# Adding the last two units' states in PSUM instead of with GpSimd, with passes re-ordered, in a 16-image conv and state-space kernel

## The chip, the core and the metric

The program runs on one core of a Trainium2 chip. The time is the device time of one execution in microseconds. The kernel before took 3897.47 us in the median of three runs (3894.95 to 3903.98).

Engines are named as the profile names them: PE is TensorE, DVE is VectorE, ACT is ScalarE, POOL is GpSimd, and SP is the queue that issues the DMAs.

## The reference

There are 16 images of 256 channels and 32 x 32 points. Two layers are applied, each with a group normalisation in front and a residual sum behind:

```python
x = x + _L0_conv_ref(_gn(x), ...)   # a 7x7 depthwise convolution whose weights come from the image itself
x = x + _L1_conv_ref(_gn(x), ...)   # in-projection, a selective scan over three resolutions, gate, out-projection
```

The second layer projects to 128 channels (`f1`, 1024 points), halves the picture twice (`f2`, 256 points, `f3`, 64 points), and runs on each level a scan forward and one backward, with 16 states:

```python
dA = jnp.exp(delta[..., None] * A)
dBx = delta[..., None] * Bs[:, :, None, :] * xt[..., None]
h = h * da + dbx                       # for every point, 16 states
y = jnp.einsum('bdn,bn->bd', h, c) + xt * Dv
return _layernorm(y, g, be)            # over the 128 channels
```

The sum of the three levels is multiplied by `silu(z)` and projected back to 256 channels.

## The kernel before

Three images are in work at once. While image i is scanned, image j = i + 1 has its 7 x 7 convolution done on PE, and image m = i + 2 is loaded, normalised, and its convolution weights are found. `stages` writes this as a body of 37 units (k = 0 to 36) and a `bridge` between two bodies; the body of images 0 to 13 is one loop of 14 turns (`Fori`, L1610), with two bodies ahead of it and two behind. Every engine runs its own instructions in the order in which they are written, and waits on semaphores for the others. So the order in `unit`, `bridge` and `tail` of each engine, and the tables at L1544 to L1551, are the schedule.

A unit is a piece of the scan. Unit 0 is the 64-point level with all 16 states and both directions; units 1 to 4 are the 256-point level, four states each and both directions; units 5 to 20 are the 1024-point level forward, one state each, and units 21 to 36 backward. A product q is a unit in one direction: 42 in all, q = 40 and 41 are units 35 and 36. In a unit of the 1024-point level:

- SP loads the rows B and C of the state, spread over all partitions, 512 KB each, into `bb` (two buffers) and `cb` (three) (`get_b`, `get_c`). `get_b` of unit k waits for POOL's `bx` pass of unit k - 2, `get_c` waits until the products of unit k - 3 are weighed.
- POOL makes `bx = bb * u` (L1466). It does so one unit ahead.
- ACT makes the decays `exp(delta * A)` in the PSUM tile `slot_b`, in two halves (`decay`, L1283).
- DVE scans each half into `slot_c` (L598) and multiplies it with `cb` into `h`, one of three places (`weigh`, L607).
- POOL adds `h` onto the sum `y` of its direction (`gather`, L1501) one unit later.

In units 1 to 4 the second direction is weighed by POOL (L1478), and PE adds the weighed states through the centring matrix `cen` into PSUM (`flat_add`, L923). For the 1024-point level `norm_centre` (L907) multiplies `y` with `cen` when all is added: parts 4 and 5 of the normalisation are the two halves of the backward direction. They stand at the head of the bridge, since they need product 41, and write into `slot_b` and `slot_c`.

Between the scan's instructions stand: on PE the 98 taps of the convolution of image j, six matmuls each (L842), of which the first seven are made in the last unit and the bridge; on ACT the 14 rows of 14 diagonal matrices for these taps (`make_row`, L1161), the copies `keep_x` (L1181) and `copy_x` (L1188), and the chunks of `delta`; on DVE the statistics of the new image (`a_s0`, L466). `delta` and `u` are made in six chunks: PE projects (`chunk_bc`, `chunk_dt`), ACT copies the rows B and C out and starts a softplus (`chunk_rows` L1228, `chunk_exp` L1236 to L1243), DVE corrects it (`chunk_first` L534), ACT takes a logarithm (`chunk_log` L1249), DVE ends it (`chunk_last` L543, L545) and POOL adds (`chunk_low` L1436, L1438). Chunks 0 and 1 are in the bridge, 2 and 3 in units 0 to 3, 4 and 5 in units 11 to 16.

The bridge gives ACT also `y_start` (L1263, five passes that start `y` with `f * Dv`, the last thing before the loop's jump) and DVE the two `output` passes (L681), `silu_clip` (L550), and unit 0's scans.

## Time and profile before

| | |
|---|---|
| median of 3 runs | 3897.47 us |
| the profiled execution | 3897.22 us, of it the span 3895.4 us |
| mean granted PE clock | 0.896 of full |
| PE busy | 3129.9 us, 80% |
| DVE busy | 3016.8 us, 77% |
| ACT busy | 2696.6 us, 69% |
| POOL busy | 3086.7 us, 79% |
| from one loop turn to the next | 228 to 232 us |

In the rows further down the first number is the start in us from the start of the span, the second the time taken, then engine, line, operation and tiles, then how many instructions are merged. What stands in brackets is how long the engine had been idle before, and what ended that; "issue" is time in which it waited for nothing that the profile shows. A matmul of 32-bit numbers is recorded as two. Busy shares near 80% on three engines say that no engine alone is the bound: each is idle at some places, and the rows show which.

### The profile page before, as it was taken

What the parts mean: (1) busy time and instruction counts of PE and PEld (TensorE: products, weight loads), DVE (VectorE), ACT (ScalarE), POOL (GpSimd) and SP (SyncE); (2) the same over time, 40 slices, a digit from 0 to 9 for tenths busy, and PEclk for the clock granted to TensorE, in tenths of its full rate; (3) what the DMA queues carried; (4) which work ended last, traced back from release to release, by engine and by line L of the source; (5) the groups of instructions that cost most, each with busy time, mean ns of one, the idle gap of its engine ahead of it and who ended that gap; (6) DMA issues with size and microseconds to landing.
All of it is one profiled execution on the core that took longest, in us unless ns stands there. A gap on an engine that the chain in (4) does not pass through costs nothing.

```text
span 3895.4 us, 54301 instructions
## 1 busy us (share of the span) xinstructions
PE 3129.9 (80%) x13644; PEld 1584.7 (41%) x13644; DVE 3016.8 (77%) x3847; ACT 2696.6 (69%) x6662; POOL 3086.7 (79%) x1588
## 2 busy tenths in 40 slices
PE   6988887987878898788888878898787879878632
PEld 3544344443434444344444434444443444443210
DVE  1058788787888878788887888788788887888887
ACT  4467676767777687776768767676776767676542
POOL 0049789796978979798796978879697897969797
PEclk8999898998898999899999989899898989989765
DMA  1026455564555546454564645455464555636454
GB/s 45 1 99 212 165 181 184 181 206 140 202 168 180 200 156 207 155 193 163 186 212 142 210 147 196 168 193 204 139 213 160 185 179 180 208 132 215 166 197 166
DMA packets 187326, 665.46 MB, mean 171 GB/s; under 512 B 22736, under 2 KB 24672, under 8 KB 186976
## 3 DMA queue, kind: packets, MB, share of 16 engines
q1 hardware_dynamic: 186976, 661.47, 50.0%
q8 instruction: 137, 2.24, 0.3%
q14 instruction: 213, 1.74, 0.2%
HBM read 639.76 MB, written 21.63 MB: 170 GB/s over the span
## 4 chain that ended last, share of the span: by engine, by line
PE 21%; POOL 21%; issue 20%; ACT 16%; DVE 12%; DMA 8%; DVEq 1%; POOLq 1%; SPq 0%; ACTq 0%
PE pconv L842 12%; POOL bx L1466 11%; DMA bb<-bc_rows 8%; POOL y L1501 7%; ACT diag L1161 5%; DVE h L607 4%; DVE slot_c L598 3%; PE pm L851 2%; PE pm L923 2%; ACT slot_b L1283 2%; PE pm L869 1%; ACT a L1274 1%; POOL h L1496 1%; POOL delta L1436 1%; ACT es L1236 1%
## 5 line engine op out<-in xcount | busy, mean ns | idle before, releaser
L842 PE MATMUL pconv<-pad,diag 128*128 128x464 f16 (+11 forms) x9408 | 2083.3, 376 | 166.8 <-DVE xn L520 99.8
L842 PEld LDWEIGHTS pconv<-pad,diag 128*128 128x128 f16 x9408 | 919.7, 99 | 1312.9 <-issue 288.4
L1501 POOL TENSOR_TENSOR y<-y,h 128x1024 f32<-128x1024 f32 (+1 forms) x544 | 1229.4, 2260 | 153.0 <-DVE h L607 149.2
L1283 ACT ACTIVATE slot_b<-delta,nega 128x512 f32<-128x512 f32 (+1 forms) x1280 | 809.6, 641 | 746.2 <-DVE slot_c L598 608.4
L1466 POOL TENSOR_TENSOR bx<-bb,u 128x1024 f32<-128x1024 f32 x512 | 1220.4, 2385 | 9.7 <-DMA bb<-bc_rows 9.0
L598 DVE TENSOR_TENSOR_SCAN slot_c<-slot_b,bx 128x512 f32<-128x512 f32 (+1 forms) x768 | 783.9, 1043 | 225.1 <-POOL bx L1466 144.8
L607 DVE TENSOR_TENSOR h<-slot_c,cb 128x512 f32<-128x512 f32 x1152 | 773.2, 672 | 0.0
L598 DVE TENSOR_TENSOR_SCAN slot_c<-slot_b,slot_c,bx 128x512 f32<-128x512 f32 x512 | 663.2, 1295 | 67.4 <-ACT slot_b L1283 9.6
L1161 ACT ACTIVATE diag<-id,chi 128x128 f16<-128x128 f16 x1568 | 496.1, 387 | 9.0 <-PE pconv L842 9.0
L1161 ACT ACTIVATE diag<-id,clo 128x128 f16<-128x128 f16 x1568 | 496.1, 387 | 0.0
L923 PE MATMUL pm<-h,cen 128*128 128x256 f32 x1024 | 251.1, 389 | 12.9 <-POOL h L1478 6.5
L1469 POOL TENSOR_TENSOR bx<-bb,u 128x1024 f32<-128x1024 f32 x64 | 157.8, 2467 | 109.6 <-DMA bb<-bc_rows 108.3
L1478 POOL TENSOR_TENSOR h<-h,cb 128x1024 f32<-128x1024 f32 x64 | 150.8, 2357 | 98.1 <-DVE h L598 98.1
L923 PEld LDWEIGHTS pm<-h,cen 128*128 128x128 f32 x1024 | 195.7, 194 | 72.0 <-DVE h L607 16.4
L1436 POOL TENSOR_TENSOR delta<-delta,rs 128x512 f32<-128x512 f32 (+1 forms) x96 | 97.9, 1020 | 155.6 <-DVE rs L545 155.5
L598 DVE TENSOR_TENSOR_SCAN h<-slot_b,bx 128x256 f32<-128x256 f32 x256 | 161.5, 672 | 53.8 <-POOL y L1501 27.0
L893 PE MATMUL pm<-f,wdelta 128*128 128x512 f32 (+1 forms) x192 | 102.6, 619 | 85.7 <-ACT rows L1228 66.6
L1446 POOL TENSOR_TENSOR f<-f,lnw 128x98 f32<-128x98 f32 x16 | 6.2, 391 | 173.5 <-ACT f L1106 173.5
L851 PE MATMUL pm<-xg,wf 128*128 128x512 f32 x128 | 94.9, 911 | 54.2 <-ACT xg L1209 54.2
L746 PE MATMUL pconv<-sg,grp 128*128 128x8 f32 x32 | 9.3, 365 | 149.9 <-DVE sg L466 149.9
L883 PE MATMUL pm<-f,wbc 128*32 128x512 f32 (+1 forms) x192 | 93.2, 570 | 25.6 <-DVE o L641 13.7
L543 DVE TENSOR_TENSOR pm<-pm,rs 128x512 f32<-128x512 f32 x64 | 44.3, 692 | 86.7 <-ACT pm L1249 86.7
(182 smaller groups left out, 3250.1 us busy)
## 6 DMA issues: line engine op xcount, KB each, us to landing
bb<-bc_rows SPq DMA_DIRECT2D x592, 512.0 KB, 4.6
cb<-bc_rows SPq DMA_DIRECT2D x592, 512.0 KB, 4.4
xr<-in_x SPq DMA_DIRECT2D x16, 1024.0 KB, 5.0
out<-ob SPq DMA_DIRECT2D x16, 1024.0 KB
bc_rows<-rows SPq DMA_DIRECT2D x64, 64.0 KB, 3.2
w<-in_w SPq DMA_DIRECT2D x2, 256.0 KB
wc<-in_wc SPq DMA_DIRECT2D x2, 256.0 KB
bc_rows<-rows SPq DMA_DIRECT2D x16, 32.0 KB, 4.5
```

The lines of the kernel that those rows point to most:

```text
L598: ins = nc.vector.tensor_tensor_scan(hv, av, bv, start, ALU.mult, ALU.add)
L607: nc.vector.tensor_tensor(half(h[:, q % HR], b), bank(slot_c, b), half(cb[:, k % CR], b), ALU.mult).then_inc(q_pr.sem, 1)
L842: ins = nc.tensor.matmul(img(bank(pconv, k), W)[:, r0:r1, c0:c1], w, pad[:, t, part, 16 * k + r0 + dy:16 * k + r1 + dy, c0 + dx:c1 + dx], ...
L851: ins = nc.tensor.matmul(bank(pm, k), wf[:, t, :], bank(xg[:, t, :], k), start=(t == 0), stop=(t == CT - 1))
L923: ins = nc.tensor.matmul(pm[:, d * L2:(d + 1) * L2], cen[:, :], h[:, q % HR, n * L2:(n + 1) * L2], start=False, stop=n == 3 and q == FLAT[-1])
L1161: ins = nc.scalar.activation(diag[:, r % RING, m, dx, :], id16[:, :], ACT.Copy, scale=(chi, clo)[m][:, t, dy * KK + dx:dy * KK + dx + 1])
L1283: ins = nc.scalar.activation(slot_b[:, o:o + w], delta[:, so + c:so + c + w], ACT.Exp, scale=nega[:, st, n0 + n:n0 + n + 1])
L1436: pool.tensor_tensor(delta[:, s:s + n], delta[:, s:s + n], er[:, c % 2, 0:n], ALU.add).then_inc(ch_delta.sem, 1)
L1466: ins = pool.tensor_tensor(bx[:, k % 2, :], bb[:, k % BR, :], us, ALU.mult)
L1469: ins = pool.tensor_tensor(o, bb[:, k % BR, :].rearrange("p (m l) -> p m l", m=m), us[:, None, :].to_broadcast([P, m, ln]), ALU.mult)
L1478: pool.tensor_tensor(h[:, q % HR, 0:HW], h[:, q % HR, 0:HW], cb[:, k % CR, :], ALU.mult).then_inc(p_pr.sem, 1)
L1501: pool.tensor_tensor(yv, yv, src[:, 0] if len(src.shape) == 3 else src, ALU.add).then_inc(q_y.sem, 1)
```

## The change

PE takes over the last two products. `gather` on POOL no longer adds q = 40 and 41. `norm_centre` of parts 4 and 5 multiplies `y`, then `h` of product 40, then `h` of product 41 with `cen`, into the same PSUM place. The rest is order:

- SP: `get_b` and `get_c` of unit 2 stand in the bridge ahead of the output's DMA, no more in unit 0 behind it; the load of the next image (`xr`) goes from unit 2 to unit 5, behind `get_c` of unit 7.
- DVE: the statistics of `xr` go from unit 3 to units 8 and 9, half each; the passes of chunk 4 are one unit later.
- PE: `lower(j, 1)` and chunk 0's projections come ahead of the second convolution tap of the last unit.
- ACT: seven diagonals of row 0 one unit later, behind `decay` of unit 36; five diagonals of row 1 out of the last unit into the bridge behind `copy_z`; `keep_x` from unit 1 to 3, `copy_x` from 1 to 4; `a_xh_` from 12 to 14; the logarithms of chunks 3 to 5 earlier within their unit (4: in unit 14).
- POOL: in unit 5 `bx` of unit 6 comes ahead of the weighing of product 9; `f_affine` in unit 26 comes one pass earlier.

```diff
+LAST = (NP - 2, NP - 1)
 def added(q):
-    return sum(v not in FLAT for v in range(q + 1))
+    return sum(v not in FLAT and v not in LAST for v in range(q + 1))
...
 (SP, unit)
-                    if k + 2 < NU:
+                    if 2 < k + 2 < NU:
                         get_b(i, k + 2)
                         get_c(i, k + 2)
-                if k == 2 and j is not None and m is not None:
+                if k == 5 and j is not None and m is not None:
                     sp.dma_start(xr[:, :, :], xv[m]).then_inc(x_in.sem, 16)
 (SP, bridge)
                     get_c(j, 1)
+                    get_b(j, 2)
+                    get_c(j, 2)
 (PE, norm_centre)
-                nc.tensor.matmul(o, cen[:, :], src, start=True, stop=True).then_inc(n_yc.sem, 1)
+                if k >= 4:
+                    pe.wait_ge(q_h.sem, q_h.at(i, NHALF))
+                    if k == 5:
+                        pe.wait_ge(q_pr.sem, q_pr.at(i, weighed(NP - 1)))
+                ins = nc.tensor.matmul(o, cen[:, :], src, start=True, stop=k < 4)
+                if k >= 4:
+                    for q in LAST:
+                        pe.wait_ge(q_pr.sem, q_pr.at(i, weighed(q)))
+                        ins = nc.tensor.matmul(o, cen[:, :], h[:, q % HR, c0:c0 + n], start=False, stop=q == LAST[-1])
+                ins.then_inc(n_yc.sem, 1)
 (ACT, bridge, behind copy_z)
                 if m is not None:
+                    make_row(m, 1, 9)
                     make_row(m, RING - 2, 0, KK)
 (ACT, unit)
-                    if k == 1:
+                    if k == 3:
                         keep_x(i)
-                if j is not None and k == 1:
+                if j is not None and k == 4:
                     copy_x(j)
 (POOL, unit)
+                    if k == 5:
+                        inputs(i, k + 1)
                     for q in products_of(k - 1):
                         if q in POOLED:
                             weigh(i, q)
-                    if k + 1 < NU:
+                    if k + 1 < NU and k != 5:
                         inputs(i, k + 1)
...
-                            if q not in FLAT:
+                            if q not in FLAT and q not in LAST:
                                 gather(i, q)
...
-pre = {3: a_s0, 18: a_max_, ...}
+pre = {8: a_s0, 9: a_s1, 18: a_max_, ...}
-CHUNK_FIRST = {(1, -4): 2, (2, -1): 3, (13, -1): 4, (15, -1): 5}
-CHUNK_LOG = {2: 3, 13: 4, 15: 5}
+CHUNK_FIRST = {(1, -4): 2, (2, -1): 3, (14, -2): 4, (15, -1): 5}
+CHUNK_LOG = {2: 3, 15: 5}            # chunk 4: at the head of unit 14
```

On PE at the head of the bridge stood, from the projection of the 64-point level on (`f` and `wc`) to chunk 1 (`wbc` with 256 columns):

```order
L869 MATMUL pm<-f,wc 128x64 [waits b_f]
L869 MATMUL pm<-f,wc 128x64 x3
L875 REGISTER_ALU
L883 MATMUL pm<-f,wbc 32x64 [waits b_f]
L893 MATMUL pm<-f,wdelta 128x64
L903 REGISTER_ALU
L907 MATMUL slot_b<-y,cen 128x512 [waits q_y]
L907 MATMUL slot_c<-y,cen 128x512 [waits q_y]
L877 ISA
L883 MATMUL pm<-f,wbc 32x256 [waits ch_rows]
```

With the change a convolution tap (`pconv`, its last two of six matmuls are shown) stands between chunk 0 and the centring, and the centring has six matmuls:

```order
L850 MATMUL pconv<-pad,diag 128x13x30
L850 MATMUL pconv<-pad,diag 128x16x30
L911 REGISTER_ALU
L916 ISA [waits q_y]
L919 MATMUL slot_b<-y,cen 128x512 [waits q_h]
L922 REGISTER_ALU
L923 MATMUL slot_b<-h,cen 128x512 [waits q_pr]
L922 REGISTER_ALU
L923 MATMUL slot_b<-h,cen 128x512 [waits q_pr]
L919 MATMUL slot_c<-y,cen 128x512 [waits q_pr,q_h,q_y]
L923 MATMUL slot_c<-h,cen 128x512 [waits q_pr] x2
L885 ISA
```

Chunk 1's projection (L883, now L891) stands behind four more matmuls.

On ACT in the bridge, from the 64-point level's decays (`a`) over `copy_z` (`sz`) to the diagonals of row 2 (`diag` from `chi`):

```order
L1274 ACTIVATE a<-delta,nega 128x64 x15
L1219 REGISTER_ALU [waits b_g]
L1220 ACTIVATE sz<-pm,vec 128x1024 [waits b_proj]
L1161 ACTIVATE diag<-id,chi 128x128 [waits row_done]
L1161 ACTIVATE diag<-id,chi 128x128 x6
```

And with the change, where the five `clo` diagonals of row 1 come in between:

```order
L1290 ACTIVATE a<-delta,nega 128x64 x15
L1235 REGISTER_ALU [waits b_g]
L1236 ACTIVATE sz<-pm,vec 128x1024 [waits b_proj]
L1177 ACTIVATE diag<-id,clo 128x128 x5
L1177 ACTIVATE diag<-id,chi 128x128 [waits row_done]
L1177 ACTIVATE diag<-id,chi 128x128 x6
```

All that follows on ACT, `y_start` with it, is five instructions further back, and five fewer stand ahead of chunk 0.

On ACT in unit 1 and 2, from the end of chunk 3's softplus start (`pm` from `es`) to its logarithm (`pm` from `pm`):

```order
L1243 ACTIVATE pm<-es 128x512 [waits ch_pos,ch_exp]
L1181 ACTIVATE xc<-xn 128x2048 [waits ob_ready]
L1187 REGISTER_ALU [waits b_xc]
L1188 ACTIVATE xn<-xr 128x2048 [waits b_xg]
L1279 REGISTER_ALU
L1283 ACTIVATE slot_b<-delta,nega 128x256 [waits q_h]
L1283 ACTIVATE slot_b<-delta,nega 128x256
L1161 ACTIVATE diag<-id,clo 128x128 x3
L1156 REGISTER_ALU
L1161 ACTIVATE diag<-id,chi 128x128 [waits row_done]
L1161 ACTIVATE diag<-id,chi 128x128 x2
L1249 ACTIVATE pm<-pm 128x512 [waits ch_err]
```

And with the change:

```order
L1259 ACTIVATE pm<-es 128x512 [waits ch_pos,ch_exp]
L1295 REGISTER_ALU
L1299 ACTIVATE slot_b<-delta,nega 128x256 [waits q_h]
L1299 ACTIVATE slot_b<-delta,nega 128x256
L1265 ACTIVATE pm<-pm 128x512 [waits ch_err]
L1177 ACTIVATE diag<-id,clo 128x128 x3
L1172 REGISTER_ALU
L1177 ACTIVATE diag<-id,chi 128x128 [waits row_done]
```

The logarithm of chunk 3 has only one `decay` ahead of it; the two copies and six diagonals that stood there come behind.

## Rows read from the trace of the kernel before

**Rows 1.** The timeline of DVE, `silu_clip` of three loop turns: start, us, line

```profile
1160.48 1.28 DVE L550 TENSOR_SCALAR o<-pm,vec 128x1024 f32<-128x1024 f32 x1
...
1392.48 1.28 DVE L550 TENSOR_SCALAR o<-pm,vec 128x1024 f32<-128x1024 f32 x1
...
1621.26 1.28 DVE L550 TENSOR_SCALAR o<-pm,vec 128x1024 f32<-128x1024 f32 x1
```

**Rows 2.** The timeline of PE from the last unit to unit 1

```profile
1373.37 1.34 PE L842 MATMUL pconv<-pad,diag 128*128 128x390 f16 x6
...
1376.45 1.08 PE L907 MATMUL slot_b<-y,cen 128*128 128x512 f32 x2
1377.36 1.02 PE L907 MATMUL slot_c<-y,cen 128*128 128x512 f32 x2
...
1388.17 1.88 PE L938 MATMUL slot_b<-o,wo 128*128 128x512 f32 x4
...
1399.25 1.98 PE L842 MATMUL pconv<-pad,diag 128*128 128x406 f16 x6 [3.13 <-issue]
...
1410.43 1.02 PE L893 MATMUL pm<-f,wdelta 128*128 128x512 f32 x2
```

**Rows 3.** The timeline of ACT, bridge to unit 13

```profile
1375.80 1.56 ACT L1161 ACTIVATE diag<-id,clo 128x128 f16<-128x128 f16 x5
...
1399.53 3.26 ACT L1263 ACTIVATE y<-f,vec 128x1024 f32<-128x1024 f32 x5
...
1466.64 0.59 ACT L1228 ACTIVATE rows<-pm 32x512 f32<-32x512 f32 x1 [1.27 <-PE pm L883]
...
1477.55 2.36 ACT L1142 ACTIVATE xh<-xr,sa 128x1024 f32<-128x1024 f32 x2
```

**Rows 4.** The timeline of DVE, units 1 to 13

```profile
1406.33 1.27 DVE L598 TENSOR_TENSOR_SCAN h<-slot_b,bx 128x256 f32<-128x256 f32 x2 [2.35 <-POOL y L1501]
...
1422.02 0.70 DVE L543 TENSOR_TENSOR pm<-pm,rs 128x512 f32<-128x512 f32 x1 [4.32 <-ACT pm L1249]
...
1429.23 2.44 DVE L466 BATCH_NORM_STATS2 sa<-xr 128x6 f32<-128x512 f32 x4
...
1477.65 0.69 DVE L534 SCALAR_TENSOR_TENSOR rs<-pm,es 128x512 f32<-128x512 f32 x1 [2.62 <-ACT pm L1243]
...
1482.38 0.70 DVE L543 TENSOR_TENSOR pm<-pm,rs 128x512 f32<-128x512 f32 x1 [2.26 <-ACT pm L1249]
```

**Rows 5.** The timeline of POOL, end of a body to unit 13

```profile
1372.65 3.19 POOL L1501 TENSOR_TENSOR y<-y,h 128x1024 f32<-128x1024 f32 x1 [0.23 <-DVE h L607]
...
1399.94 2.73 POOL L1469 TENSOR_TENSOR bx<-bb,u 128x1024 f32<-128x1024 f32 x1 [7.03 <-DMA bb<-bc_rows]
...
1439.91 4.68 POOL L1466 TENSOR_TENSOR bx<-bb,u 128x1024 f32<-128x1024 f32 x2
...
1447.42 2.36 POOL L1466 TENSOR_TENSOR bx<-bb,u 128x1024 f32<-128x1024 f32 x1 [0.51 <-DMA bb<-bc_rows]
...
1485.69 2.35 POOL L1501 TENSOR_TENSOR y<-y,h 128x1024 f32<-128x1024 f32 x1 [3.48 <-DVE h L607]
```

**Rows 6.** A window (PE, PEld, DVE, ACT, POOL, clock, DMA, GB/s); `bb`'s landings

```profile
1420.00:1428.00 8.00, 8.00 (x38) 4.97 (x36) 5.95 (x10) 6.52 (x20) 4.98 (x4) 1.00 0.93 328
...
DMA to landing us min/median/max: 3.3/4.6/7.2
```

**Rows 7.** The timeline of PE at slow jumps, then DVE behind one

```profile
937.96 2.43 PE L842 MATMUL pconv<-pad,diag 128*128 128x406 f16 x6 [5.87 <-issue]
...
3008.40 2.43 PE L842 MATMUL pconv<-pad,diag 128*128 128x406 f16 x6 [4.38 <-issue]
...
1185.07 1.27 DVE L598 TENSOR_TENSOR_SCAN h<-slot_b,bx 128x256 f32<-128x256 f32 x2 [3.61 <-PE pm L923]
```

**Rows 8.** PE at the end of the last image; then the window there, columns as in rows 6

```profile
3876.01 2.08 PE L907 MATMUL slot_b<-y,cen 128*128 128x512 f32 x2 [22.56 <-POOL y L1501]
...
3876.00:3881.00 5.00, 4.99 (x6) 2.11 (x7) 0.00 (x0) 1.19 (x2) 0.00 (x0) 0.50 0.00 0
```

More of the change, by code:

```diff
@@ L461, in _, with stats @@
             dve.wait_ge(setup, DVE_SET + ACT_SET)
-            def stats(b, s, x, done):
-                for t in range(CT):
+            def stats(s, x, ts):
+                for t in ts:
                     for k in range(2):
                         ins = nc.vector.bn_stats(s[:, 12 * t + 6 * k:12 * t + 6 * k + 6], bank(x[:, t, :], k))
-                ins.then_inc(done.sem, 1)
+                return ins
             def a_s0(m):
@@ L471, in a_s0, with a_s1 @@
                 dve.wait_ge(x_in.sem, x_in.at(m + 1, 0))
-                stats(m, sa, xr, a_stats)
+                stats(sa, xr, (0,))
+            def a_s1(m):
+                stats(sa, xr, (1,)).then_inc(a_stats.sem, 1)
             def low_half(j, t):
@@ L1006, in unit @@
                         lower(j, 0)
-                    if m is not None:
-                        taps(m, BRIDGE_TAPS[1], BRIDGE_TAPS[2])
-                    if j is not None:
                         lower(j, 1)
@@ L1012, in unit @@
                         chunk_dt(j, 0)
+                    if m is not None:
+                        taps(m, BRIDGE_TAPS[1], BRIDGE_TAPS[2])
                 if m is not None and k in pre:
@@ L1355, in tail @@
                     make_row(m, 0, 0, KK)
-                if k == PREP + 1:
-                    if j is not None:
-                        b_normal(j)
+                if j is not None and k == PREP + 1:
+                    b_normal(j)
+                if k == PREP + 2:
                     if m is not None:
                         make_row(m, 0, KK)
-                if k == PREP + 2:
-                    if m is not None:
                         prep(m, 1)
@@ L1374, in tail @@
                         copy_f(j, 2)
-                    if m is not None:
-                        make_row(m, 1, 9)
             def unit(i, j, m, k):
@@ L1382, in unit @@
                 if i is not None:
[L1383 to L1384 removed]
+                    if k in (1, 14):
+                        chunk_log(i, {1: 2, 14: 4}[k])
                     if k == 11:
@@ L1390, in unit @@
                         decay(i, k + 1, 0)
+                    if k in CHUNK_LOG:
+                        chunk_log(i, CHUNK_LOG[k])
                 if m is not None and k == PREP:
@@ L1515, in unit @@
                             weigh(i, q)
-                    if k + 1 < NU:
+                    if k + 1 < NU and k != 5:
                         inputs(i, k + 1)
+                if m is not None and k == 26:
+                    f_affine(m)
+                if i is not None:
                     for v in (k - 1, k) if k == NU - 1 else (k - 1,):
                         for q in products_of(v):
-                            if q not in FLAT:
+                            if q not in FLAT and q not in LAST:
                                 gather(i, q)
```

16 lines of the change are left out of this document (5 added, 11 removed).

## The prediction

> **What bounds the kernel now.** I read the timelines of one loop turn, engine by engine, with what ended each idle time; shares of the whole span do not help, since the bound changes within a turn. First DVE's `silu_clip`, which stands once in each turn: the turns are 232.0 and 228.8 us long [rows 1], so there are two kinds. I work through the short one from 1392 on and return to the long one.
>
> In units 7 to 33 POOL is the bound: two passes of about 2.35 us per unit back to back, with one hole of 3.48 us at unit 14 [rows 5], where DVE comes late because it stood idle 2.62 and 2.26 us for ACT's chunk 4 [rows 4]. ACT in turn came late there: its copy of the rows waited 1.27 us for PE, and 2.36 us of `xh` stood before its next work [rows 3]. So PE's place in its own queue matters at unit 11, through ACT. In the bridge and units 0 to 5 no engine is full. PE runs without a hole from the centring at 1376.45 to the jump, after which 3.13 us pass; POOL's last `y` ends at 1372.65 + 3.19 = 1375.84, 0.6 us before the centring starts [rows 2, 5]. So POOL's last two passes are hardly what the bridge waits for: PE got there only then. DVE then waits 2.35 us for POOL's first `y`, which needs `y_start`, ended on ACT at 1399.53 + 3.26 = 1402.8, and 4.32 us for the logarithm of chunk 3 [rows 3, 4].
>
> **The bridge: a loss.** The two POOL passes go, but what replaces them stands on the engine that is full. Four matmuls more: two in a row start 0.91 us apart [rows 2], 4 x 0.91 = 3.6 us. From below nothing is excluded only if PE has a hole there, and it has none; from above, each could take the 2.08 us that the pair at the granted clock of 0.50 took in the last image [rows 8], 8.3 us. I take 3.6, because the same place ran at 0.91. The tap that moves in front of the centring takes about 1.2 us (1.34 less the overlap into the next), of which 0.4 comes back because the 64-point projection no longer stands behind it [rows 2]: 0.8. Out-projection and everything behind it on PE start 3.6 + 0.8 = 4.4 us later, DVE's outputs too, since they wait for it. The stall that the change removes for POOL, 7.03 us for the third `bb` of the bridge [rows 5], was in front of work that waited for `y_start` anyway: worth nothing. `decay` of unit 36 comes 2.0 us earlier on ACT (seven diagonals less ahead), and the last product with it: nothing behind it waits for it any more, so nothing.
>
> On ACT the bridge's chain hangs on PE's spread, so +4.4; the five diagonals of 1.56 us [rows 3] now stand ahead of `y_start`, where before they filled a wait; about 0.8 us comes back from DVE's chunk 1 pass, which then runs without a POOL pass beside it. `y_start` ends at 4.4 + 1.6 - 0.8 = 5.2 us later, POOL's first `y` follows, and DVE's scan at 1406.33 [rows 4] starts 5.2 us later.
>
> **Units 1 to 6: a gain of the same size.** The logarithm of chunk 3 stood on ACT behind two copies (3.8 us) and six diagonals (1.9 us). Now it has one `decay` ahead, and 4.32 us of DVE's wait [rows 4] go; 0.5 to 0.9 us of other small waits in these units are absorbed by the lateness. Unit 3 starts on DVE at +0.2. The statistics, 2.44 us in unit 3 [rows 4], no longer stand ahead of the scans for which POOL waits; and in unit 5 `bx` of unit 6 comes ahead of a weighing, so it comes about 2.5 us earlier than 1439.91 [rows 5]. POOL's sum of passes is the same, so its `bx` of unit 8 would be free to start at 1446.6 instead of 1447.42 [rows 5].
>
> It has to wait for its data, though. `get_c` of unit 7 waits for the weighing of product 9, now behind one pass more (+2.1 us), then the 1 MB of `xr` is issued, and only then `get_b` of unit 8. In the window with `xr` in it the queues moved 328 GB/s at a DMA share of 0.93 [rows 6]; 1 MB in front costs 3.2 us more. The 512 KB take 4.6 us as a rule, and 7.2 at most [rows 6]. Issued at 1443.2, they land at about 1450: +2.7 us against 1447.42.
>
> PE is late too. Chunk 3's projection (1410.43, [rows 2]) moves by 4.2; of it PE gets back 0.8 in small holes until unit 5, then it has none until unit 13: +3.4 at unit 10 and 11, where ACT waited for it already [rows 3].
>
> **Units 8 to 16: the lateness is paid back.** ACT's rows of chunk 4 at 1466.64 come 3.4 us later. `xh` (2.36 us) stands two units further back, the logarithm too, and DVE asks for chunk 4 a unit later, so its waits of 2.62 and 2.26 us go, 4.9 us. The moved statistics cost DVE 2.44 us in units 8 and 9, hidden by its slack against POOL. Followed through: ACT's chunk 5 comes 0.9 us earlier than before, DVE's unit 16 at -0.2, and POOL has two holes of about 0.8 instead of one of 3.48. POOL's `bx` of unit 18 starts at 3.48 - 2.7 - 0.8 + ~0.2 = -0.2 us. From there to the bridge nothing changes. A turn is worth -0.2 us, 14 turns -3 us. It is the difference of about 8 us lost and 8 us won; each part is good to 1 us, the whole to 3.
>
> **The long turns.** Where the jump cost PE 4.4 to 5.9 us instead of 3.1 to 3.6 (five of 14), DVE waited 3.61 us for PE in unit 2 [rows 7], and the turn was about 3.1 us longer. At the jump 2 MB are under way: output, third `bb` and `cb`. With the change the latter two have landed. If that is what slows the jump, up to 5 x 3.1 = 15.5 us go; if not, none. I take half, -8.
>
> **The last images.** Images 14 and 15 have no diagonals and no statistics: the bridge's loss comes with less to gain, +3 in all. At the very end PE adds 40 and 41 itself; its `y` part can start before product 41 is weighed: -2.3 for the POOL pass, + two to three matmuls at the low clock, between 0 and +4; I take 0.5.
>
> The Trainium skill, page "TensorE: Matmul & The Clock Gate", Part 1, says that the throttled clock is the default and activity releases it; the trace agrees, PE comes out of 22.56 us of idleness at a granted clock of 0.50 [rows 8]. By that rule the added matmuls cost double in the last image only, since in the loop's bridge PE comes to them at work, and its pair stood 0.91 us apart [rows 2]; the sum would be the same.
>
> The page "GPSIMD Engine Reference", section "Specifications", says that GpSimd shares its SBUF interfaces with VectorE when that has two SBUF inputs. The trace agrees: the `y` pass beside such a DVE pass took 3.19 us, another 2.35 [rows 5]. By it the early third `bx` runs against DVE's 64-point scans and lengthens them by about 1 us, ahead of a wait of 3 us: nothing in the sum.
>
> **The sum.** The profiled execution took 3897.22 us, 1.8 us more than its span, and is 0.25 us under the median. 3897.2 - 3 - 8 + 3 + 0.5 = 3889.7; I say 3890.
>
> **The rivals.**
> Slower: the repayment in units 8 to 16 fails. ACT starts its work for chunk 4 3.4 us late, POOL 2.7 us late; if DVE's waits there come back in another place (for chunk 5, or for the decays behind `xh` in unit 14), the hole of 3.48 us stays and the turn is 3.0 us longer: 14 x 3.0 + 3.5 = +45, 3942; decided from where ACT ends chunk 5's start later than before. For it: ACT has no hole between units 11 and 13, and PE's lateness goes straight into it. Against it: 2.9 us of ACT's work leave that stretch. Half of it gives 3920.
>
> Clearly faster: PE's lateness is not there, because PE's jump is short and the rest of its waits in units 0 to 5 (0.8 us and those for POOL's weighed states) hold more slack than I found. Then the whole hole of 3.48 goes, the turn is worth -2.5 to -3, and long turns vanish: -14 x 2.5 - 8 = 3854. Against it: PE is full from 1412 on.
>
> No gain in the long turns and none in the short: the two POOL passes were off the path, so the change doesn't do what it says; the rest cancels: 3897 to 3901.
>
> **How the numbers follow.** The forecast's own range is 3875 to 3903, chance 0.4; slower 0.27; clearly faster 0.18; no change at all 0.15. What a measurement of this kernel tells from no change is about 0.2%, 8 us. The forecast lies at its edge: of its 0.4, 0.23 is faster, 0.12 the same, 0.05 slower. Faster 0.23 + 0.18 + 0.02 = 0.43, same 0.12 + 0.11 = 0.23, slower 0.05 + 0.27 + 0.02 = 0.34. The range 3850 to 3936 leaves out a tenth at either end.
>
> **What would show it.** Right if: PE's out-projection comes 4 to 5 us later after the last unit; the five diagonals stand before `y_start`, and DVE waits about 3 us for POOL's first `y` (2.35 before); no wait of DVE for `pm` L1249 of chunk 3; POOL's hole before `bx` of unit 8 is 3 us or more; DVE's two waits at chunk 4 are gone and the POOL hole at unit 14 is under 2 us; fewer turns over 231 us. Wrong if the centring starts earlier than 0.5 us before its old place, if `bx` of unit 8 waits for nothing, or if ACT comes to unit 14 as late as to unit 11.

## The result, and the profile after

The changed kernel took 3935.15 us (median of 5 runs, 3933.52 to 3940.14) against 3898.51 us for the kernel before beside it: a ratio of 1.0086, 95% interval 1.0072 to 1.0100. On another chip, later, the same kernel took 3933.39 us against 3914.85, a ratio of 1.0039 (1.0023 to 1.0054). (The ratios are worked out from all executions, so they are not the quotients of the medians.) It is slower both times; what is known of why the ratio differs stands below. The forecast was 3890 us and slightly faster. The time lies at the upper end of its range, and the sign was wrong.

The page of the profile after, its first lines and the groups of GpSimd and VectorE that answer to the prediction (line engine op, count, busy and mean ns, idle before and its releaser):

```profile
span 3938.3 us, 54525 instructions
...
PE 3220.4 (82%) x13772; PEld 1622.5 (41%) x13772; DVE 3008.5 (76%) x3847; ACT 2694.4 (68%) x6662; POOL 2995.9 (76%) x1556
...
L1479 POOL TENSOR_TENSOR bx<-bb,u 128x1024 f32<-128x1024 f32 x512 | 1222.6, 2388 | 69.5 <-DMA bb<-bc_rows 69.4
L1514 POOL TENSOR_TENSOR y<-y,h 128x1024 f32<-128x1024 f32 (+1 forms) x512 | 1143.4, 2233 | 63.0 <-DVE h L615 59.3
L606 DVE TENSOR_TENSOR_SCAN slot_c<-slot_b,bx 128x512 f32<-128x512 f32 (+1 forms) x768 | 783.6, 1043 | 260.4 <-POOL bx L1479 227.4
L1509 POOL TENSOR_TENSOR h<-h 128x512 f32<-128x512 f32 (+3 forms) x128 | 86.8, 678 | 147.0 <-ACT y L1279 139.5
L1449 POOL TENSOR_TENSOR delta<-delta,rs 128x512 f32<-128x512 f32 (+1 forms) x96 | 98.1, 1022 | 377.1 <-DVE rs L553 377.1
```

POOL is 76% busy and less than before, since its two passes per image are gone, and the kernel is slower: the idle time in front of `delta` rose from 155.6 us to 377.1, by more than the 86 us of the passes that are gone, in a place where POOL waits for the bridge anyway. Of the 69.4 us in front of `bx` only 9.0 were there before.

`silu_clip` again, which stands once in each turn:

```profile
1409.29 1.27 DVE L558 TENSOR_SCALAR o<-pm,vec 128x1024 f32<-128x1024 f32 x1
...
1641.43 1.28 DVE L558 TENSOR_SCALAR o<-pm,vec 128x1024 f32<-128x1024 f32 x1
```

A turn is 232.14 us long where the short turn was 228.8 [rows 1]. Over the 14 turns the median is 232.2, with three of 234.3 to 235.1. The mean, 232.75, is 2.7 us over that of before (230.04, short and long turns together): 14 x 2.7 = 38 us. The last body is 3.3 us longer too; the first `silu_clip` comes 2.9 us later (243.12 against 240.21), and what follows the last one is 1.2 us shorter: 43 us between the two spans. The 2.9 us are not shown to be the change's: in a later profile of the same kernel (after2) the first `silu_clip` stands at 239.84.

In what follows 12.7 us are taken off times of the changed kernel's turn at 1371 to 1603 to lay it on the turn of rows 1 to 5: GpSimd's pass for `y` that waits 2.92 us for `h` stands at 1371.27 in one and 1358.57 in the other.

TensorE in the bridge:

```profile
1388.71 1.34 PE L850 MATMUL pconv<-pad,diag 128*128 128x390 f16 x6
1389.89 1.02 PE L919 MATMUL slot_b<-y,cen 128*128 128x512 f32 x2
1390.74 1.88 PE L923 MATMUL slot_b<-h,cen 128*128 128x512 f32 x4
1392.46 1.02 PE L919 MATMUL slot_c<-y,cen 128*128 128x512 f32 x2
1393.32 1.88 PE L923 MATMUL slot_c<-h,cen 128*128 128x512 f32 x4
1395.13 0.62 PE L891 MATMUL pm<-f,wbc 128*32 128x256 f32 x2
...
1404.99 1.88 PE L955 MATMUL slot_b<-o,wo 128*128 128x512 f32 x4
...
1415.88 2.43 PE L850 MATMUL pconv<-pad,diag 128*128 128x406 f16 x6 [2.95 <-issue]
```

The added matmuls take 1392.46 - 1390.74 = 1.72 and 1395.13 - 1393.32 = 1.81 us, 3.5 together. The out-projection stands at 1404.99 - 12.7 = 1392.3, 4.1 us later than before [rows 2]; 4.4 was forecast.

GpSimd from unit 7 on:

```profile
1464.70 2.35 POOL L1479 TENSOR_TENSOR bx<-bb,u 128x1024 f32<-128x1024 f32 x1 [4.74 <-DMA bb<-bc_rows]
...
1504.93 2.36 POOL L1514 TENSOR_TENSOR y<-y,h 128x1024 f32<-128x1024 f32 x1 [0.62 <-DVE h L615]
...
1574.74 0.37 POOL L1465 TENSOR_TENSOR wlo<-wg,whi 128x98 f16<-128x98 f32 x1 [1.32 <-ACT whi L1140]
```

The hole of 3.48 us at unit 14 [rows 5] is down to 0.62 here (0.87 in the median of the 14 turns), as forecast. In its place there are two others: 4.74 us for `bb` of unit 8, and 1.32 for ACT's `whi` in unit 28.

### The profile page after: what moved, and what is told of

Same layout as the page of the kernel before. It is cut to its first block, busy times and chain, and to the rows that moved or that the text cites. A ratio compares the mean times of both kernels' runs of the same rounds, so it can differ in the third digit from the quotient of the medians.

```text
span 3938.3 us, 54525 instructions
## 1 busy us (share of the span) xinstructions
PE 3220.4 (82%) x13772; PEld 1622.5 (41%) x13772; DVE 3008.5 (76%) x3847; ACT 2694.4 (68%) x6662; POOL 2995.9 (76%) x1556
## 4 chain that ended last, share of the span: by engine, by line
PE 23%; POOL 23%; issue 18%; DMA 12%; DVE 11%; ACT 11%; DVEq 1%; SPq 1%; POOLq 0%; ACTq 0%
POOL bx L1479 13%; DMA bb<-bc_rows 12%; PE pconv L850 11%; POOL y L1514 7%; DVE h L615 4%; ACT diag L1177 3%; DVE slot_c L606 3%; PE pm L859 2%; PE pm L940 2%; ACT a L1290 1%; PE pm L877 1%; POOL h L1491 1%; DVE h L606 1%; PE pm L891 1%; ACT slot_b L1299 1%
## 5 line engine op out<-in xcount | busy, mean ns | idle before, releaser
L850 PE MATMUL pconv<-pad,diag 128*128 128x464 f16 (+11 forms) x9408 | 2123.1, 381 | 123.8 <-DVE xn L528 67.6
L850 PEld LDWEIGHTS pconv<-pad,diag 128*128 128x128 f16 x9408 | 931.1, 101 | 1288.1 <-issue 320.1
L1479 POOL TENSOR_TENSOR bx<-bb,u 128x1024 f32<-128x1024 f32 x512 | 1222.6, 2388 | 69.5 <-DMA bb<-bc_rows 69.4
L1514 POOL TENSOR_TENSOR y<-y,h 128x1024 f32<-128x1024 f32 (+1 forms) x512 | 1143.4, 2233 | 63.0 <-DVE h L615 59.3
L1449 POOL TENSOR_TENSOR delta<-delta,rs 128x512 f32<-128x512 f32 (+1 forms) x96 | 98.1, 1022 | 377.1 <-DVE rs L553 377.1
L1509 POOL TENSOR_TENSOR h<-h 128x512 f32<-128x512 f32 (+3 forms) x128 | 86.8, 678 | 147.0 <-ACT y L1279 139.5
L891 PE MATMUL pm<-f,wbc 128*32 128x512 f32 (+1 forms) x192 | 92.5, 566 | 58.7 <-DVE o L649 45.6
```

The source lines that it names most:

```text
L850: ins = nc.tensor.matmul(img(bank(pconv, k), W)[:, r0:r1, c0:c1], w, pad[:, t, part, 16 * k + r0 + dy:16 * k + r1 + dy, c0 + dx:c1 + dx], ...
L891: nc.tensor.matmul(bank(pm, 1 if c == 5 else 0)[0:2 * NS, 0:n], wbc[:, st, :], f[:, fc:fc + n], start=True, stop=True).then_inc(ch_bc.sem, 1)
L1479: ins = pool.tensor_tensor(bx[:, k % 2, :], bb[:, k % BR, :], us, ALU.mult)
L1514: pool.tensor_tensor(yv, yv, src[:, 0] if len(src.shape) == 3 else src, ALU.add).then_inc(q_y.sem, 1)
```

## The experiments

A turn's length tells more than a ratio of medians, since the kernel before took between 3898 and 3921 us by the chip. So each trial has both; the turn is the median of the 14 distances between `silu_clip`s in its profile, with the mean behind it. In several kernels turns come in two lengths; there the median jumps from one to the other, and the mean is the better guide. Where kernels of different chips are compared, a few microseconds prove nothing.

| kernel | turn, us: median, mean | median time, us | ratio to before beside it |
|---|---|---|---|
| before, and again as before2 | 229.2, 230.0; 232.2, 232.0 | 3898.5; 3915.8 | 1; 0.9986 |
| changed (two chips) | 232.2, 232.8; 232.4, 233.0 | 3935.2; 3933.4 | 1.0086; 1.0039 |
| b_last | 233.4, 233.7 | 3961.6 | 1.0126 |
| a_pooladd | 228.8, 229.4 | 3881.8 | 0.9913 |
| a_xrearly | 229.4, 230.1 | 3903.9 | 0.9985 |
| a_unswap | 230.4, 230.6 | 3901.6 | 0.9969 |
| a_wlow29 | 231.4, 231.3 | 3920.0 | 1.0010 |
| a_tinyxr | 231.7, 230.9 | 3910.5 | 0.9997 |
| a_taps | 231.6, 231.3 | 3918.6 | 1.0003 |
| c_early | 226.7, 226.9 | 3850.4 | 0.9827 |
| c_early_wlo | 225.3, 225.5 | 3834.7 | 0.9795 |
| c_unswap_wlo | 225.3, 225.6 | 3832.7 | 0.9785 |
| d_diag | 225.3, 225.3 | 3828.7 | 0.9782 |
| d_early | 225.3, 225.5 | 3832.7 | 0.9791 |
| d_taps | 224.5, 224.3 | 3816.4 | 0.9748 |
| e_taps_diag | 224.1, 224.0 | 3812.6 | 0.9734 |
| b_load | 228.7, 229.1 | 3887.7 | 0.9925 |

**The matmuls alone, and all but the matmuls.** The first is the kernel before with this alone (`LAST` and `added` as in the change):

```diff
+                if k >= 4:
+                    for q in LAST:
+                        pe.wait_ge(q_pr.sem, q_pr.at(i, weighed(q)))
+                        ins = nc.tensor.matmul(o, cen[:, :], h[:, q % HR, c0:c0 + n], start=False, stop=q == LAST[-1])
...
-                            if q not in FLAT:
+                            if q not in FLAT and q not in LAST:
                                 gather(i, q)
```

> The kernel before with one part of the change alone: TensorE adds the states of units 40 and 41 in PSUM, GpSimd's two passes go, nothing is re-ordered. Theory (the bridge's loss is the four added matmuls and carries through, because GpSimd is full from unit 5 on and nothing here takes away its hole of 3.48 us at unit 14): about +3.6 us in the bridge, all of it kept, 14 x 3.6 = +50, near 3948 us; at least +30. Rival (the added matmuls are covered, and the loss of the changed kernel comes from its re-ordering alone): within 10 us of the kernel before, 3890 to 3908.

The second is the changed kernel with this, and the waits of `norm_centre` that hang on it:

```diff
-LAST = (NP - 2, NP - 1)
+LAST = ()
```

> The changed kernel with its re-ordering kept, but units 40 and 41 added by GpSimd again as before (two passes more, four matmuls less). Theory (matmuls cost 3.6 us per turn in the bridge, on the path): TensorE's out-projection, VectorE's outputs and everything to unit 8 come about 3.6 us earlier, 14 x 3 to 3.6 = -42 to -50 us, 3885 to 3893 us, faster than the kernel before. Rival (the loss sits in the burst of transfers at unit 8 and in the wait for wlo, the matmuls are covered): 3930 to 3940, as the changed kernel.

Both went as the theory had it: b_last stands 1.3% over the kernel before, which is the +50 us expected, though on a chip where the kernel before itself took 3912.9 us; a_pooladd is 53 us under the changed kernel, a little more than the 42 to 50. Two rows of `silu_clip`, first of b_last, then of a_pooladd:

```profile
1409.49 1.28 DVE L553 TENSOR_SCALAR o<-pm,vec 128x1024 f32<-128x1024 f32 x1
...
1641.58 1.27 DVE L553 TENSOR_SCALAR o<-pm,vec 128x1024 f32<-128x1024 f32 x1
```

```profile
1388.06 1.28 DVE L558 TENSOR_SCALAR o<-pm,vec 128x1024 f32<-128x1024 f32 x1
...
1616.83 1.28 DVE L558 TENSOR_SCALAR o<-pm,vec 128x1024 f32<-128x1024 f32 x1
```

With the matmuls alone a short turn is 232.1 us, 3.3 over 228.8. Without them the changed kernel has short turns of 228.8, 3.4 less than with them. So the exchange costs nearly the whole length of the matmuls (3.5 us) in both surroundings, and the two POOL passes give next to nothing back. The re-ordering by itself leaves a short turn exactly as long as it was. The forecast had it win 3.8 us.

**The transfer of xr.** Three trials on the changed kernel. SyncE's queue in the changed kernel itself:

```profile
1455.34 0.32 SPq L403 DMA_DIRECT2D cb<-bc_rows  x1
1455.92 0.39 SPq L432 DMA_DIRECT2D xr<-in_x  x1
1456.42 0.40 SPq L403 DMA_DIRECT2D bb<-bc_rows  x1
1456.93 0.41 SPq L403 DMA_DIRECT2D cb<-bc_rows  x1
1457.66 0.32 SPq L403 DMA_DIRECT2D bb<-bc_rows  x1
```

Three megabytes are asked for within 2.3 us. The first four of these transfers stood behind one wait for POOL's weighing, which ends at 1455.3; the last was let go by the `bx` pass that ends at 1457.6. The `bb` at 1456.42 is the one for which POOL waits; it lands 8.1 us later (7.8 to 8.7 over the 14 turns). First, `xr` out before the wait:

```diff
                 if 2 < k + 2 < NU:
                     get_b(i, k + 2)
+                if k == 5: ... xr ...
                     get_c(i, k + 2)
-                if k == 5: ... xr ...
```

> The changed kernel with one transfer in another place: xr (1 MB) is issued between get_b(7) and get_c(7), so as soon as copy_x has read it (1452.0 in the changed kernel's trace) instead of behind get_c(7) at 1455.9. Theory (bb of unit 8 landed 8.5 us after its issue because xr was put out 0.5 us ahead of it): it lands 4.6 to 6 us after its issue at about 1455.9, GpSimd's wait of 4.74 us falls to 1.0 to 2.5, and 2 to 3.5 us per turn are won: 3888 to 3908 us. Rival (bb of unit 8 is bound by something else, or TensorE's lateness takes over at unit 11): under 1 us per turn, 3921 to 3935.

Second, POOL's passes of unit 5 in their old order:

```diff
-                    if k == 5:
-                        inputs(i, k + 1)
                     for q in products_of(k - 1):
...
-                    if k + 1 < NU and k != 5:
+                    if k + 1 < NU:
```

> The changed kernel with the exchange on GpSimd in unit 5 undone: the weighing of unit 5 runs ahead of bx of unit 6 again. Then get_c(7), and what stands behind it on the queue (xr, bb of unit 8), is no longer held by the pass in between: get_c(7) and xr 2.3 us earlier, bb of unit 8 0 to 1 us earlier (it then waits for bx of unit 6 itself). Theory (the exchange made the burst): GpSimd's wait for bb of unit 8 falls by 1 to 2.5 us, 3900 to 3921 us. Rival (the burst is xr's alone and the exchange is neutral, VectorE's scan of unit 6 then waits longer for bx): 3930 to 3945.

Third, `xr` in its place with 8 of its 1024 columns per half, which leaves out nearly all of this input:

```diff
-                    sp.dma_start(xr[:, :, :], xv[m])
+                    sp.dma_start(xr[:, :, 0:8], xv[m][:, :, 0:8])
```

> The changed kernel with xr's transfer in its place, but 8 KB of it in place of 1 MB (the rest of xr keeps what it held, so this input is left out). Theory (most of GpSimd's 4.74 us for bb of unit 8 is the megabyte ahead of it, the rest the late issue behind get_c(7)): the wait falls to 1 to 2 us, 2.8 to 3.5 us per turn, 3885 to 3898 us. Rival (the late issue at 1456.4 alone does it, three transfers at once being slow anyway): it stays above 3.5 us, 3920 to 3935 us.

The pass that waits, of the three in this order:

```profile
1678.03 2.36 POOL L1479 TENSOR_TENSOR bx<-bb,u 128x1024 f32<-128x1024 f32 x1 [2.10 <-DMA bb<-bc_rows]
```

```profile
1441.79 2.36 POOL L1479 TENSOR_TENSOR bx<-bb,u 128x1024 f32<-128x1024 f32 x1 [1.49 <-DMA bb<-bc_rows]
```

```profile
1450.04 2.35 POOL L1479 TENSOR_TENSOR bx<-bb,u 128x1024 f32<-128x1024 f32 x1 [2.75 <-DMA bb<-bc_rows]
```

The 4.74 us fall to 2.10, 1.49 and 2.75. The first two confirm the place of the loss and bring 2.8 and 1.8 us per turn by the medians. By the means it is 2.6 and 2.1 us, by the times 2.2 and 2.4, so the two remedies are worth the same within what can be told. In a_unswap the wait fell by 3.2 us, more than the 1 to 2.5 expected: `bb` goes out 1.1 us earlier (46.0 instead of 47.1 us behind `silu_clip`), and lands in 5.9 us though `xr` is still 1.7 us ahead of it.

The third misses both expectations: without its megabyte the wait is 2.0 us shorter, not 2.8 to 3.5, and `bb` still takes 6.1 us to land (5.0 to 7.5 by the turn), with `cb`, `bb` and `cb` issued within two microseconds. With both remedies together (d_early, further down) it lands in 4.4 us and POOL does not wait. From these differences I estimate three parts of the wait: the megabyte (2.0 us), the other transfers close by (6.1 - 4.4 = 1.7) and the later issue (1.1).

The mean turn of a_tinyxr is 1.9 us shorter than that of the changed kernel, which is the 2.0 us of the wait; its median hides it. Five of its turns are 228.8 to 229.1 us and nine 231.3 to 232.4. In the five POOL does not wait for `wlo` at all; in eight of the nine it waits 1.34 to 1.41 us. That is part of the difference; the rest I did not follow.

**wlo.** One unit later:

```diff
-                    if k == 28:
+                    if k == 29:
                         w_low(m)
```

> The changed kernel with GpSimd's small pass for wlo one unit later (29 instead of 28), behind two more passes of 2.35 us. Theory (wlo's wait of 1.32 us for ACT's whi is on GpSimd's path in each turn, as nothing but GpSimd sets the pace there): the wait goes and the turn is 1.3 us shorter, 14 x 1.3 = 18 us, 3910 to 3925 us. Rival (the wait is covered: VectorE or TensorE at the end of the turn sets the time, and the hole appears again as a longer wait of 2.92 us for VectorE's h at unit 32): 3930 to 3938.

The turn is 0.8 us shorter by the median and 1.45 by the mean, the time 15 us shorter than the changed kernel's 3935 (and 13 than its 3933): most of the 18 us expected. The clearer proof is the next pair.

**Do the terms add?**

> The changed kernel with GpSimd adding units 40 and 41 again, and xr issued ahead of get_c(7): both losses removed, the re-ordering kept. Theory (the two losses are separate terms of one sum): the gain of the one (about 4 us per turn, measured) and the gain of the other (2.8 us per turn, measured) add, turns of about 226 us, ratio to the kernel before 0.9913 - 0.0101 = 0.981, 3820 to 3830 us at 3898 for before. Rival (a turn has a floor of 228.7 us that another engine sets, since short turns of the kernel before and of both single trials have that length): 3855 to 3875.

> As the last, with the pass for wlo in unit 29 too. Theory (terms add): 1.3 us per turn less, ratio about 0.976, 3800 to 3815 us. Rival (the floor of 228.7 us per turn): 3850 to 3875; a rival between them: TensorE comes nearer to the end of GpSimd's turn and only half of it shows, 3815 to 3830.

> The changed kernel with GpSimd adding units 40 and 41, the exchange of passes in unit 5 undone instead of the earlier xr, and wlo in unit 29. Theory: GpSimd still waits about 1.5 us for bb of unit 8 (as with the exchange alone undone) against 2.1 with the earlier xr: within 10 us of the last kernel, 3800 to 3820 us. Rival (the earlier bx of unit 6 is worth something to VectorE): 10 us or more slower than it.

They add, nearly. `xr` early takes a_pooladd's 228.8 to 226.7, `wlo` in unit 29 takes that to 225.3: 2.1 and 1.4 us. The ratio of c_early is the 0.981 expected within its interval; c_early_wlo came to 0.9795 (0.9771 to 0.9820) where full addition gave 0.976, so some microseconds of the sum are missing. All three took longer than their ranges in microseconds, which had been worked out for a kernel before of 3898 us; beside them it took 3917. There is no floor of 228.7 us; that several kernels had turns of that length was chance. The old order in unit 5 is worth as much as the early `xr`.

**What else the re-ordering holds.** Three edits to c_unswap_wlo: the five diagonals of row 1 back in the last unit, `xr` early too, TensorE's bridge in its old order:

```diff
                         lower(j, 0)
+                    if m is not None:
+                        taps(m, BRIDGE_TAPS[1], BRIDGE_TAPS[2])
+                    if j is not None:
                         lower(j, 1)
                         chunk_bc(j, 0)
                         chunk_dt(j, 0)
-                    if m is not None:
-                        taps(m, BRIDGE_TAPS[1], BRIDGE_TAPS[2])
```

> The fastest kernel so far (changed kernel, GpSimd adds 40 and 41, exchange in unit 5 undone, wlo in unit 29) with the five diagonals of row 1 back from the bridge to the last unit. Theory (they stand ahead of y_start for 1.6 us, and GpSimd's first y pass waits 9.2 us for y_start): VectorE's scan in the bridge comes 1.2 to 1.6 us earlier, and about 1 us of it per turn is kept, 10 to 20 us faster than 0.9785 of the kernel before, a ratio of 0.974 to 0.976. Rival (they delay ScalarE's chunk 0 at the end of the turn by as much, where it stands between VectorE's two chunk passes): 0.978 to 0.982.

> The fastest kernel so far with xr issued ahead of get_c(7) too. Theory (the remaining 1.5 us of wait for bb of unit 8 is xr's megabyte directly ahead): xr goes out about 1.5 to 2 us earlier, the wait falls below 0.8 us, 0.5 to 1.3 us per turn, ratio 0.974 to 0.977. Rival (bb of unit 8 is issued when bx of unit 6 is done and the wait is its own landing): within 5 us of 0.9785.

> The fastest kernel so far with TensorE's order in the bridge as in the kernel before: three taps between the two projections of lower, so one tap less ahead of the centring and the taps ahead of chunk 0's projections. Theory (the new order is worth nothing or a little: the tap in front cost 0.8 us, chunk 0 comes earlier): within 0.5 us per turn, ratio 0.977 to 0.981. Rival (the new order carries a large part of the gain, since chunk 0's start on ScalarE and VectorE is on the bridge's chain): 1.5 us or more per turn slower, ratio above 0.984.

The diagonals and the second remedy for `xr` gave nothing that can be told from the interval (0.9782 and 0.9791 against 0.9785). For `xr` the profile says why. POOL's wait for `bb` of unit 8 (1.6 us in the median of c_unswap_wlo) is gone, and some 20 us later POOL waits as long for DVE:

```profile
1430.57 1.27 DVE L471 BATCH_NORM_STATS2 sa<-xr 128x6 f32<-128x512 f32 x2
...
1435.47 1.27 DVE L471 BATCH_NORM_STATS2 sa<-xr 128x6 f32<-128x512 f32 x2
...
1444.97 2.35 POOL L1514 TENSOR_TENSOR y<-y,h 128x1024 f32<-128x1024 f32 x1 [1.57 <-DVE h L615]
```

From 1418 to 1444 DVE has no hole above 0.3 us: the statistics that the change moved to units 8 and 9, with the normalisation passes beside them, fill it. TensorE's order, which I had expected to be worth nothing, gave 0.8 us per turn by the median and about 1.2 by the mean and by the time (16 us). One tap in front of the centring was put at 0.8; the edit also moves the taps against chunk 0's projections, so how much is the tap's is not told apart. That was tried on the changed kernel too, and the diagonals again without that tap:

> The changed kernel itself again, on the chip of the next two. The kernel before took 3898 to 3917 us by the chip, so a difference between single trials of other calls is good to 0.4% only. Theory: turns of 232.1 us with a few longer ones whatever the chip, 3930 to 3942 us, ratio 1.004 to 1.009. Rival (the change gets its whole 0.9% from the first chip, on which the kernel before had fewer long turns): ratio under 1.004.

> The changed kernel with TensorE's order in the bridge as before (one tap less ahead of the centring, three taps between the two projections of lower), the rest changed. Theory (the new order costs the 0.8 us of the tap in front and delays what hangs on the centring, as it did in the fast version, where undoing it won 0.4%): 0.5 to 1.3 us per turn, 7 to 18 us faster than the changed kernel. Rival (in the changed kernel its cost is covered by GpSimd's other waits): within 4 us of it.

> The fastest kernel (GpSimd adds 40 and 41, exchange in unit 5 undone, wlo in unit 29, TensorE's bridge as before) with the five diagonals of row 1 back in the last unit too. Theory (undoing the diagonals won 4 us, not beyond its interval; with TensorE's order undone ScalarE's start of y is next on the chain): 0.5 to 1 us per turn more, 3802 to 3812 us. Rival (covered): 3812 to 3820 us.

On one chip the old order makes the changed kernel 15 us faster (3918.6 against 3933.4), within the 7 to 18 expected. The diagonals bring 0.4 us per turn now by the profiles of two chips; the intervals of the two ratios overlap (0.9717 to 0.9751 and 0.9727 to 0.9770), so this gain is not shown. At 3812.6 us it stands between theory and rival. e_taps_diag is the fastest kernel of all, 2.7% under the kernel before. It keeps the change's other moves: the earlier logarithm and later chunk 4, `xh` in unit 14, the statistics in units 8 and 9, `bb` and `cb` of unit 2 in the bridge.

**The long turns.** The kernel before again, and with the third loads of the bridge alone ahead of the output:

```diff
                     get_b(j, 1)
                     get_c(j, 1)
+                    get_b(j, 2)
+                    get_c(j, 2)
                 if i is not None:
                     sp.wait_ge(ob_ready.sem, ob_ready.at(i + 1, 0))
```

> The kernel before itself with a profile, beside the next. On its first chip 6 of its 14 turns took 230.5 us or more. Theory (its time by the chip, 3898 to 3917 us, is the number of long turns, 3.1 us each): at 3910 us or more it has 8 to 12 long turns, short ones still of 228.3 to 229.3. Rival (all its turns are longer on another chip): short turns above 229.5 us.

> The kernel before with one part alone: bb and cb of unit 2 are asked for in the bridge, ahead of the output, instead of behind it in unit 0. Theory of the forecast (the long turns come from a loop jump under the load of output, third bb and cb): the long turns go, up to 3.1 us each, 15 to 30 us faster than before2. Rival (the long turns are set by TensorE's own place relative to what it waits for, not by these transfers): as many as in before2, within 6 us of it.

In this profile all 14 turns of the kernel before are long, 230.9 to 232.8 us; I had expected 8 to 12, and short ones beside them. The profiled execution is the slowest of ten (3925.0 us; their median is 3915.8), so in most of the others some turns will have been short. With the loads moved, 12 of 14 turns are 228.2 to 229.3, and the kernel is 28 us faster by the medians (0.9925, interval 0.9903 to 0.9948), within the 15 to 30 expected. A short turn is as long as in the kernel before (228.7 and 228.8), so the gain is not that `bb` lands earlier. TensorE behind the loop's jump, of before2 and of b_load in the same turn:

```profile
713.28 2.43 PE L842 MATMUL pconv<-pad,diag 128*128 128x406 f16 x6 [6.32 <-issue]
```

```profile
704.84 2.38 PE L844 MATMUL pconv<-pad,diag 128*128 128x406 f16 x6 [3.00 <-issue]
```

The thirteen jumps take 3.8 to 6.3 us in before2, 3.1 to 5.9 in the first profile of before [rows 7], and 2.8 to 3.2 in b_load, as in the changed kernel. So most long turns of the kernel before come from jumps beside these transfers (four of the six in the first profile; the other two follow no slow jump), and the change does away with them. How many there are differs from execution to execution, and its medians differ from chip to chip, 3898 to 3921 us. This fits the loss of 0.9% on one chip and 0.4% on the other: the changed kernel's own time is the same (3935 and 3933), and the kernel before was slower beside the second. No profile of it was taken on that second chip, so its long turns there were not counted.

In the first profile of the kernel before, POOL waits 1.33 to 1.38 us for `wlo` in five of the six long turns and at most 0.42 in the short ones; in b_load it waits 1.34 in a turn of 231.8 us and at most 0.47 in the others. So this wait is part of what a long turn consists of.

There is a second kind of long turn, which the trials with short jumps still have: 3 of 14 in a_pooladd, more in some others. The same stretch of TensorE's second half in a short and in a long turn of a_pooladd (window, busy of PE, PEld, DVE, ACT and POOL, granted clock, DMA share, GB/s):

```profile
1480.00:1500.00 20.00, 16.52 (x61) 6.84 (x62) 16.16 (x20) 14.39 (x29) 18.95 (x11) 0.84 0.49 177
1500.00:1520.00 20.00, 16.37 (x85) 9.00 (x83) 18.39 (x22) 13.65 (x33) 20.00 (x10) 0.90 0.64 232
...
1938.00:1958.00 20.00, 17.37 (x59) 7.44 (x60) 16.23 (x20) 14.40 (x29) 18.88 (x11) 0.76 0.52 173
1958.00:1978.00 20.00, 16.38 (x75) 8.56 (x74) 18.34 (x22) 13.80 (x32) 20.00 (x10) 0.84 0.64 229
```

The granted clock is lower there, 0.76 and 0.84 against 0.84 and 0.90, behind a hole of 4.67 us that both turns have. Why one turn gets less than another, no run tells. That it makes the turn long was read from these rows and not tested.

## Why the prediction was wrong, step by step

**The bridge, right.** 3.6 us for the matmuls (3.5 in the trace, 3.3 to 3.4 in two trials), 0.8 for the tap (0.8 to 1.2 in d_taps, with what else its edit moves), outputs 4.4 later (4.1). That the POOL passes were not on the path held in both trials. The diagonals in front of `y_start` were put at 1.6 us; undoing them gave nothing that stands clear of the intervals. DVE waits 2.39 us for POOL's first `y`, where about 3 was the sign. The 64-point scans, said to become 1 us longer beside the early `bx`, took 5.10 us instead of 4.53. POOL's first `y`, forecast 5.2 us later, came 4.7 later:

```profile
1423.75 1.27 DVE L606 TENSOR_TENSOR_SCAN h<-slot_b,bx 128x256 f32<-128x256 f32 x2 [2.39 <-POOL y L1514]
```

1423.75 - 12.7 = 1411.05 against 1406.33 [rows 4].

**Units 1 to 6, right up to the transfer.** The wait of 4.32 us for chunk 3's logarithm [rows 4] is gone. POOL is free for `bx` of unit 8 at 1464.70 - 4.74 - 12.7 = 1447.3, 0.7 us after the forecast.

**The landing of bb for unit 8, the first step that failed.** The forecast has two terms, 3.2 us for the megabyte and 4.6 for the transfer, from an issue at 1443.2. They make 7.8 and a landing at 1451.0; the text says about 1450, +2.7 us, which is 6.8 and drops a microsecond. The issue came at 1443.7 and the landing took 8.1: `bx` at 1452.0, +4.6 us. Of the 1.9 us between, 1.0 is that slip in the sum, 0.5 the later issue, and 0.3 the landing. That the landing itself is so near 7.8 is luck, since both terms were off: the megabyte costs 2.0, and without it `bb` takes 6.1, because the step asked what stands directly ahead of the transfer and not what else is let go beside it.

**Units 8 to 16, right in the main.** The rival for "slower" was that this lateness isn't repaid at chunks 4 and 5. ACT's copy of the rows of chunk 4 waited 1.33 us for PE, much as before [rows 3], and came 5.0 us later than before (3.4 was forecast). But DVE's waits of 2.62 and 2.26 us [rows 4] are down to this one, and 0.56 us for a decay behind it:

```profile
1495.46 0.69 DVE L542 SCALAR_TENSOR_TENSOR rs<-pm,es 128x512 f32<-128x512 f32 x1 [0.62 <-ACT pm L1259]
```

POOL's hole of 3.48 us is 0.62 too. The rival's own sign, ACT ending the start of chunk 5 later than before, did come (by 0.5 us, where 0.9 earlier was forecast), but the hole did not stay. So the time came out near that rival's 3942, but not by its mechanism.

**"From there to the bridge nothing changes", the second step that failed.** From unit 14 on POOL runs closer behind PE and ACT than before, because its hole there went and theirs did not. In unit 28 it meets their chain for the weights of the next image:

```profile
1570.06 0.49 ACT L1131 ACTIVATE wg<-pm,vec 128x49 f32<-128x49 f32 x2 [2.95 <-PE pm L804]
```

ACT waits for PE's product, and `wlo` on POOL for ACT: 1.32 us, 1.4 by the trial. The matmuls are not to blame: a_pooladd has the same wait (1.38). Nor is it new: before2 has 1.34 to 1.38 us there in nine of its 14 long turns. I had seen that wait in a long turn and had not asked when a short one would get it.

**The sum.** Forecast for a short turn: 3.6 + 0.8 + the rest, -0.2. Measured: +3.3. The two failed steps, 4.6 - 2.7 = 1.9 and 1.3 to 1.4, are 3.3 of the 3.5 us between. The second term is the weaker one: in after2 four turns have no wait for `wlo` and are as long as the others (231.6 to 232.6 us); in three of them POOL had waited 5.5 to 6.0 us for `bb` of unit 8, where 4.8 is the median. So the two overlap in part.

**The long turns, right in mechanism.** The forecast counts five turns behind jumps of 4.4 to 5.9 us; the profile has four, and two more long turns without one. I gave half of 15.5 us to it; on the first chip the mean of the turns stands 1.25 us above a short turn in before and 0.6 in the changed kernel, which has three longer turns beside short jumps: 14 x 0.65 = 9 us, the forecast's 8. On the chip of before2 it was worth more: b_load took 28 us less. The sign "fewer turns over 231 us" did not come: all 14 are over it, since the short turn itself is 232.

**The end.** Forecast +3 and +0.5. The last body is 3.3 us longer; behind its `silu_clip` 213.7 us pass to the end instead of 214.9.

```profile
3917.22 2.04 PE L919 MATMUL slot_b<-y,cen 128*128 128x512 f32 x2 [19.07 <-DVE slot_c L606]
3919.06 2.88 PE L923 MATMUL slot_b<-h,cen 128*128 128x512 f32 x4
...
3922.64 1.88 PE L923 MATMUL slot_c<-h,cen 128*128 128x512 f32 x4
```

Out of 19 idle microseconds the first pair takes 2.04 us as in the kernel before [rows 8], the first two added matmuls 2.88 and the other two 1.88 (a row counts each float32 matmul twice): only the start is at the lower clock. Two windows (columns as in [rows 6]) show it:

```profile
3919.00:3921.00 2.00, 2.00 (x4) 0.90 (x3) 0.00 (x0) 0.00 (x0) 0.00 (x0) 0.50 0.00 0
3921.00:3924.00 3.00, 3.00 (x8) 1.32 (x8) 0.00 (x0) 0.60 (x1) 0.00 (x0) 0.99 0.00 0
```

The granted clock is 0.50 (1.2 GHz) up to 3921 and 0.99 (2.4 GHz) behind it. The Trainium skill, page "TensorE: Matmul & The Clock Gate", Part 1, says that the throttled clock is the default and that activity releases it; the trace agrees.

## What to carry to other kernels

Work taken from an engine that waits at that place anyway gave nothing here, and the same work on the engine that is full there cost nearly all of its time: look at what the other engine does in the same microseconds, not at the totals. When a wait on a DMA queue moves, list everything queued behind it, since it will be issued together, and take the landing time of such a burst rather than the median. A wait removed is worth only what the next engine lets through: with both remedies for `bb` POOL waited for DVE instead, and the time stayed. And where one engine is to gain microseconds over the others in mid-turn, follow it past each later hand-over, small ones too: a pass of 0.37 us gave back half of a hole of 3.

## What the runs showed of the hardware

The jump of TensorE at the loop's end took 2.7 to 3.4 us in all profiles in which the third loads had been asked for early, and 3.1 to 6.3 us where they were under way with the output. In one profile of the kernel before it took over 4 us in 4 of 13 turns, in another, on another chip, in 12 of 13. The medians of that kernel were 3898 to 3921 us from chip to chip, and single executions on one chip ran from 3894 to 3934; the changed kernel, with short jumps throughout, took 3935 and 3933. That the number of slow jumps accounts for this spread was not counted beyond the two profiles.

A 512 KB transfer landed in 4.6 us in the median. With others of its size issued 1.1 us ahead of it and 0.6 and 1.2 us behind it, it took 6.1 us (5.0 to 7.5 over the turns of a_tinyxr), with a megabyte 1.7 us ahead of it 5.9 (5.7 to 7.3 in a_unswap), with such neighbours and a megabyte 0.5 us ahead 8.1 (7.8 to 8.7), and with the megabyte 3 us ahead and the others 2 us away 4.4 (4.3 to 5.0 in d_early).
